# Node values moved from VectorE to GpSimd, the second norm moved into the pair tiles, the first tile's pair weights ahead of the scans

## The reference

```python
diff  = cg[:, :, None, :] - cg[:, None, :, :]
decay = exp(where(tri, diff, -1e30))
levels = floor(log2(s XOR t)) + 1, and 0 for s == t
lam_ts = Lam[t, head, levels[t, s]]          # Lam = softplus(Lp * dl)
scores = q_t . k_s / sqrt(64)
Y = (scores * decay * lam_ts) @ V
o = Y @ Wout.T + x, then a layer norm of o with ln_g, ln_b
```

## Time and profile before

| | |
|---|---|
| median of 3 runs | 1217.08 us (1216.16 to 1217.61) |
| profiled execution | 1215.93 us |
| its span | 1213.8 us |
| mean granted TensorE clock | 0.959 of full |
| TensorE busy | 1091.7 us |
| VectorE busy | 1004.4 us |
| ScalarE busy | 691.8 us |
| GpSimd busy | 310.4 us |

### The profile page before, as it was taken

One profiled execution on the slowest core, in us unless ns is written; L12 is line 12 of the kernel. 1 busy time (PEld: TensorE's weight loads), 2 busy tenths in 40 slices (PEclk: granted clock), 3 DMA queues, 4 the chain that ended last, 5 costly groups with the idle time before them and its releaser, 6 DMA issues.

```text
span 1213.8 us, 18006 instructions
## 1 busy us (share of the span) xinstructions
PE 1091.7 (90%) x5756; PEld 665.3 (55%) x5756; DVE 1004.4 (83%) x2141; ACT 691.8 (57%) x1366; POOL 310.4 (26%) x197
## 2 busy tenths in 40 slices
PE   5799989998998989899998989989898998989872
PEld 3455646555564655556465555646555564655641
DVE  4688897979979797997979799797979979797677
ACT  4483845738375573837557283755728375572761
POOL 0050320504114050411405041140504114050273
PEclk9899989899999999999899999999999999999885
DMA  3000000000000000000000000000000000001136
GB/s 133 9 9 10 1 18 9 17 9 0 17 9 17 9 17 9 0 17 9 17 9 17 9 0 17 9 17 9 17 9 0 17 9 17 9 17 54 67 101 203
DMA packets 32562, 28.64 MB, mean 24 GB/s; under 512 B 1568, under 2 KB 26144, under 8 KB 32288
## 3 DMA queue, kind: packets, MB, share of 16 engines
q1 hardware_dynamic: 32544, 28.42, 7.2%
HBM read 16.09 MB, written 12.32 MB: 23 GB/s over the span
## 4 chain that ended last, share of the span: by engine, by line
PE 45%; DVE 37%; issue 11%; ACT 5%; DMA 1%; DVEq 0%; ACTq 0%; SPq 0%; POOLq 0%; POOL 0%
DVE ms L1256 6%; PE p L581 4%; PE p L619 3%; DVE skip L1088 3%; PE p L544 3%; PE p L556 2%; PE p L570 2%; DVE pair L1329 2%; DVE nodesT L1265 2%; PE p L433 2%; PE p L394 2%; ACT vdw L849 2%; PE p L424 2%; DVE pair L1323 2%; DVE y L1168 2%
## 5 line engine op out<-in xcount | busy, mean ns | idle before, releaser
L1516 POOL TENSOR_TENSOR pair<-pair,cgt 128x2048 f32<-128x2048 f32 x16 | 58.4, 3647 | 772.5 <-DVE pair L1316 772.5
L858 ACT ACTIVATE gx<-p 128x512 f32<-128x512 f32 x256 | 143.4, 591 | 13.9 <-PE p L479 8.2
L477 PE MATMUL p<-x1Th,Gl 128*128 128x512 f32 x256 | 120.1, 469 | 4.0 <-ACT gx L858 4.0
L813 ACT ACTIVATE gelu<-p,bias_u 128x512 f32<-128x512 f32 x32 | 22.0, 687 | 151.3 <-PE p L424 151.3
L479 PE MATMUL p<-x1Th,Gh 128*128 128x512 f32 x256 | 102.1, 399 | 0.0
L478 PE MATMUL p<-x1Tl,Gh 128*128 128x512 f32 x256 | 101.8, 398 | 0.0
L1529 POOL TENSOR_TENSOR vp<-vdw,beta 128x384 f32<-128x384 f32 (+3 forms) x80 | 80.9, 1042 | 56.0 <-DVE beta L1308 56.0
L544 PE MATMUL p<-gx,x1T 128*32 128x512 f32 x512 | 77.2, 679 | 12.8 <-DVE pair L1333 12.0
L581 PEld LDWEIGHTS p<-vbd,pair 128*128 128x128 f32 x512 | 62.0, 191 | 42.9 <-issue 31.0
L1256 DVE TENSOR_TENSOR ms<-lam,K 128x64 f32<-128x64 f32 (+4 forms) x80 | 84.5, 1132 | 0.0
L394 PE MATMUL p<-xnT,MC 128*128 128x512 f32 x64 | 42.6, 756 | 46.4 <-DVE y L1161 46.4
(11 more groups left out here) (239 smaller groups left out, 2705.3 us busy)
## 6 DMA issues: line engine op xcount, KB each, us to landing
xin<-in_x SPq DMA_DIRECT2D x16, 256.0 KB, 2.8
hx_scratch<-vdw SPq DMA_DIRECT2D x16, 256.0 KB, 2.5
res_scratch<-res SPq DMA_DIRECT2D x15, 256.0 KB, 2.0
W<-in_weights SPq DMA_DIRECT2D x1, 1477.5 KB, 9.3
gx<-hx_scratch SPq DMA_DIRECT2D x5, 256.0 KB, 4.5
out<-gx SPq DMA_DIRECT2D x5, 256.0 KB, 2.7
gx<-in_weights SPq DMA_DIRECT2D x1, 1216.0 KB, 11.7
GT<-hx_scratch SPq DMA_DIRECT2D x4, 256.0 KB, 4.1
```

The costliest lines, as they stand in the source:

```text
L477: pe.matmul(head_bank(h)[:, :], tile(Gl, h), x1Th[:, :], start=True, stop=False)
L858: act.activation(tile(gx, h, T), head_bank(h)[:, :], ACT.Copy).then_inc(R["gx_copied"], 1)
```

## The change

- `pair_differences` and ScalarE's `pair_decay` work by tile, in four pieces each.
- Level 0 goes into the node values. The setup (`node_vectors`) makes `member` (query or key below the node), `rbit` and `own_coef`, and adds to `left` a row for the token itself. A new VectorE step `fold_own` combines level 0 with the levels 1 to 5 in `lam`, behind `lam_sum`. `own_level` and `self_lam` go, and with them the sum of L1329 in `pair_weights`.
- `node_lams` moves from VectorE to GpSimd: behind `pair_differences` and ahead of `level_values`, five products (1, 2, 4, 8, 16 columns) and a copy.
- `attention_out` writes into `skip` and not into `rs`. `norm2` moves from ahead of `node_rows` to behind `pair_weights(1)`.
- `pair_weights(0)` moves ahead of the scans, and TensorE's `pair_levels(0)` ahead of `left_halves`.

```diff
-        yt, ytT, ob = rs[:, 0:T], rs[:, T:2 * T], rs[:, 2 * T:3 * T]
+        yt, ytT, ob = rs[:, 0:T], rs[:, T:2 * T], skip
...
                     pair_scores(i, 0)
+                    pair_levels(i, 0)
                     left_halves(i)
-                    pair_levels(i, 0)
                     node_matrices(i)
...
+                for n in range(TILES):
+                    act.wait_ge(R["diff_ready"], 4 * i + n + 1)
+                    act.activation(tile(pair, n, 512), tile(pair, n, 512), ACT.Abs).then_inc(R["diff_abs"], 1)
+                for n in range(TILES):
+                    act.wait_ge(R["diff_abs"], 4 * i + n + 1)
+                    act.activation(tile(pair, n, 512), tile(pair, n, 512), ACT.Exp, scale=-1.0).then_inc(R["decay_ready"], 1)
...
                 if later(i):
                     act.wait_ge(R["m_ps"], 4 * i)
                 if later(i):
-                    act.wait_ge(R["n_ready"], i)
+                    act.wait_ge(R["ob_ready"], i)
+                    act.wait_ge(R["c_ready"], B if isinstance(i, int) else i)
...
+            def node_vectors():
...
+                step(dve.transpose(left_t[:, :], k("left")))
+                step(dve.tensor_reduce(member[:, :], view(left_t[:, :], "p (c n) -> p n c", c=4), AX.X, ALU.add))
+                step(dve.tensor_tensor(member[:, :], member[:, :], k("right"), ALU.add))
...
+                step(dve.scalar_tensor_tensor(own_coef[:, 0:5], ones_to[:, 1:6], -2.0, ones_to[:, 0:5], ALU.mult, ALU.add))
+                step(dve.tensor_copy(own_coef[:, 5:6], ones_to[:, 5:6]))
+                left = view(k("left"), "p (c s) -> p c s", c=4)
+                step(dve.scalar_tensor_tensor(left, spread(k("own_chunk").unsqueeze(2), [128, 4, CHUNK]), k("diag", 31, 32),
+                                              left, ALU.mult, ALU.add))
...
+            def fold_own(i):
 
                 dve.wait_ge(R["lam_ready"], i + 1)
                 if later(i):
-                    dve.wait_ge(R["lev_ps"], 4 * i)
+                    dve.wait_ge(R["nodes_ready"], i)
...
+                own = view(lam_own[:, :], "p (m l) -> p m l", l=6)
+                dve.tensor_tensor(own, spread(l[:, :, 0:1], [128, 64, 6]),
+                                  spread(own_coef[:, :].unsqueeze(1), [128, 64, 6]), ALU.mult).then_inc(R["own_steps"], 1)
+                dve.tensor_tensor(l[:, :, 1:6], l[:, :, 1:6],
+                                  spread(rbit[:, :].unsqueeze(1), [128, 64, 5]), ALU.mult).then_inc(R["own_steps"], 1)
+                dve.wait_ge(R["own_steps"], 2 * i + 2)
+                dve.tensor_tensor(l[:, :, 1:6], l[:, :, 1:6], own[:, :, 0:5], ALU.add).then_inc(R["lamx_ready"], 1)
...
             def pair_weights(i, n):
-                if n == 0:
-                    dve.wait_ge(R["decay_ready"], i + 1)
+                dve.wait_ge(R["decay_ready"], 4 * i + n + 1)
                 dve.wait_ge(R["lam_ps"], 4 * i + n + 1)
                 dve.tensor_tensor(tile(pair, n, 512), tile(pair, n, 512), P1[2][:, :], ALU.mult)\
                     .then_inc(R["dlam_ready"], 1)
 
-                if n == 0:
-                    dve.wait_ge(R["self_ready"], i + 1)
+                dve.wait_ge(R["s_ps"], 4 * i + n + 1)
                 dve.wait_ge(R["dlam_ready"], 4 * i + n + 1)
-                dve.tensor_tensor(tile(pair, n, 512), tile(pair, n, 512), tile(self_lam, n, 512), ALU.add)\
-                    .then_inc(R["lams_ready"], 1)
-                dve.wait_ge(R["s_ps"], 4 * i + n + 1)
-                dve.wait_ge(R["lams_ready"], 4 * i + n + 1)
                 dve.tensor_tensor(tile(pair, n, 512), tile(pair, n, 512), P1[1][:, :], ALU.mult)\
                     .then_inc(R["w_ready"], 1)
 
...
             def attention_out(i):
                 dve.wait_ge(R["wo_ps"], i + 1)
-                if later(i):
-                    dve.wait_ge(R["n_ready"], i)
+                dve.wait_ge(R["skip_ready"], i + 1)
...
                     lam_sum(i)
+                    fold_own(i)
...
-                    node_lams(i)
                 if j is not None:
                     scan_inputs(j)
                 if i is not None:
-                    if later(i):
-                        norm2(i - 1)
                     node_rows(i)
+                if i is not None:
+                    pair_weights(i, 0)
                 if j is not None:
                     scans(j)
                 else:
                     cell_out()
-                if i is not None:
-                    pair_weights(i, 0)
                 if j is not None:
                     top1(j)
                 if i is not None:
                     own_heads(i, 0)
                     pair_weights(i, 1)
+                    if later(i):
+                        norm2(i - 1)
...
+            def node_lams(i):
+
+                pool.wait_ge(R["lamx_ready"], i + 1)
+
+                if later(i):
+                    pool.wait_ge(R["c_ready"], B if isinstance(i, int) else i)
+                if later(i):
+                    pool.wait_ge(R["lev_ps"], 4 * i)
+                l = view(lam[:, :], "p (m l) -> p m l", l=LEVELS)
+                own = view(lam_own[:, :], "p (m l) -> p m l", l=6)
+                nd = view(nodes[:, :], "p (m n) -> p m n", n=NODES)
+                at = 0
+                for level in range(5, 0, -1):
+                    count = CHUNK >> level
+                    pool.tensor_tensor(nd[:, :, at:at + count], spread(l[:, :, level:level + 1], [128, 64, count]),
+                                       spread(member[:, at:at + count].unsqueeze(1), [128, 64, count]), ALU.mult)
+                    at += count
+                pool.tensor_copy(nd[:, :, at:at + 1], own[:, :, 5:6]).then_inc(R["nodes_ready"], 1)
...
-                pw = view(pair[:, :], "p (m t) -> p m t", t=CHUNK)
-                pool.tensor_tensor(pw, pw, spread(cgt[:, :].unsqueeze(2), [128, 64, CHUNK]), ALU.subtract)\
-                    .then_inc(R["diff_ready"], 1)
+                for n in range(TILES):
+                    pw = view(tile(pair, n, 512), "p (m t) -> p m t", t=CHUNK)
+                    pool.tensor_tensor(pw, pw, spread(cgt[:, H * n:H * n + H].unsqueeze(2), [128, H, CHUNK]), ALU.subtract)\
+                        .then_inc(R["diff_ready"], 1)
...
                 pair_differences(i)
+                node_lams(i)
                 level_values(i)
-                own_level(i)
```

More of the change, by code:

```diff
@@ L168, in build @@
         nodesT = sb("nodesT", TILES * 512)
-        self_lam = sb("self_lam", TILES * 512)
+        lam_own = sb("lam_own", 64 * 6)
+        member = sb("member", NODES)
+        left_t = sb("left_t", 128)
+        rbit = sb("rbit", 5)
+        ones_to = sb("ones_to", 6)
+        own_coef = sb("own_coef", 6)
         vp = sb("vp", 2048)
@@ L198, in build @@
         P1 = [psum(f"p1_{n}") for n in range(5)]
[L200 removed]
+        names = """loaded heads_loaded folded basis setup_ps setup_ev setup_done G_ps G_ready Gh_ready Gl_ready
             gates_xh_ready gates_xl_ready
@@ L1067, in before, with step @@
                 dve.wait_ge(R["setup_done"], 3)
+            def node_vectors():
+                steps = [0]
+                def step(ins):
+                    steps[0] += 1
+                    ins.then_inc(R["basis"], 1)
+                    dve.wait_ge(R["basis"], steps[0])
+                step(dve.transpose(left_t[:, :], k("left")))
[4 more added lines that the diff above has]
+                    count = CHUNK >> level
+                    step(dve.tensor_reduce(rbit[:, level - 1:level], k("right", at, at + count), AX.X, ALU.add))
+                    at += count
+                step(dve.memset(ones_to[:, 0:1], 1.0))
+                for level in range(1, 6):
+                    step(dve.tensor_tensor(ones_to[:, level:level + 1], ones_to[:, level - 1:level],
+                                           rbit[:, level - 1:level], ALU.mult))
+                step(dve.scalar_tensor_tensor(own_coef[:, 0:5], ones_to[:, 1:6], -2.0, ones_to[:, 0:5], ALU.mult, ALU.add))
[3 more added lines that the diff above has]
+                                              left, ALU.mult, ALU.add))
             def heads_low_part():
@@ L1468, in stages @@
                     heads_low_part()
+                    node_vectors()
                 if j is not None:
```

32 lines of the change are left out of this document (7 added, 25 removed).

## The result

The changed kernel takes 1249.82 us (median of 4 runs, 1247.48 to 1251.67) against 1217.34 us of the kernel before on the same chip. The ratio is 1.025, with a 95% interval of 1.0225 to 1.0275. The prediction was 1219.0 us, with a range up to 1234: it was wrong. The profiled execution took 1250.59 us, of which the span is 1248.8.

The account below looks back on a forecast made before the run. The prediction took the moment VectorE issues scan_inputs as the limit, with w(0) second. Its terms, 1.3 - 4 - 2 - 8.5 + 9 + 2.7 + 3.4, sum to +1.9 us: 1219.0 us, range 1191 to 1234.

Parts of the forecast that it names:

- step 9: ScalarE's Abs and Exp in four pieces add perhaps 0.8 us, vbd ready near 586.2: costs nothing.
- step 4: VectorE's alpha products wait in turns for GpSimd's node products; scan_inputs starts near 581.6 against 581.71: -2 us over 15 passes.
- Step 6: norm2 and L1329's additions leave the queue, pair_weights(0) comes earlier; TensorE's w(0) waits at L544 go: -8.5 us.
- Step 7: With pair_levels(0) ahead of left_halves, node_matrices wait 0.6 us for ScalarE's last copy in each of 15 passes: +9 us.
- Step 8: pair_levels(0) asks for nodesT earlier; with the clock up TensorE waits 0.9 us, in three passes: +2.7 us.
- Step 11: Pass 1's 6.66 us stall before the MC matmul shrinks to the other passes' 2.96, plus some clock: -4 us.
- step 10: At the start, node_vectors puts 17 waited-for instructions, 3.8 us, where 2.6 us are idle: +1.3 us.
- Step 3: GpSimd's node values, five products and a copy, take 4.5 us, from 575.0 to 579.5; bounds 3.7 and 5.3 us.
- the second rival: GpSimd's nodes are slower, 5.3 us, so beta, stats2 and scan_inputs come 0.8 us later: 1233 us, chance 0.20.
- The first rival: Node instructions do not hold VectorE in turns; scan_inputs starts at 578.4: 1188 us, or 1203 for half; chance 0.30.
- Step 5: GpSimd's level values start at 580.4, end by 585.2, before TensorE comes to left_halves after 586: hidden.
- Step 12: At the end, norm2(14) comes later, GpSimd's end sums start near 1181, and attention_out(15) is issued at 1205.7: +3.4 us.

Follow-up runs that it names:

- Experiment 1: Changed kernel with ScalarE's rstd2(i-1) moved from behind heads(12, 14) to behind own_values: 1215.43 us, ratio 0.998.
- experiment 5: Experiment 2's kernel with level_weights directly behind lam_sum on VectorE, ahead of fold_own: 1206.12 us, ratio 0.9891.
- experiment 9: Experiment 2's kernel with level_weights cut in two: beta products ahead of fold_own, alpha products and their product with e4 behind top1: 1188.23 us, ratio 0.9744.
- experiment 10: Experiment 9's kernel with ScalarE's Abs and Exp as one instruction each: 1186.79 us, ratio 0.9739.
- experiment 12: Experiment 10's kernel with the beta products between fold_own and delta, and ScalarE's own values behind its left_halves copies: 1187.79 us, ratio 0.9743.
- Experiment 8: Kernel before with only norm2(i-1) moved behind pair_weights(1), its sum written to skip's buffer, additions of self_lam kept: 1268.82 us, ratio 1.0406.
- experiment 3: Changed kernel with pair_levels(0) back behind left_halves on TensorE: 1273.80 us, ratio 1.0454.
- experiment 11: Experiment 2's kernel with pair_levels(0) back behind left_halves on TensorE and pair_weights(0) back behind the scans on VectorE: 1237.44 us, ratio 1.0154.
- experiment 2: Changed kernel with stats2(i-1) ahead of level_weights on VectorE: 1203.37 us, ratio 0.988.
- experiment 4: Changed kernel with ScalarE's Abs and Exp as one instruction of 2048 elements each instead of four of 512: 1234.96 us, ratio 1.0122.
- experiment 6: Experiment 5's kernel with level_values ahead of node_lams, left_halves ahead of pair_levels(0), and the scans ahead of pair_weights(0): 1272.47 us, ratio 1.0443.
- experiment 7: Experiment 6's kernel with ScalarE's Abs and Exp as one instruction each: 1251.19 us, ratio 1.0276.

## Why the prediction was wrong

The step that failed is step 9, "nothing" for ScalarE, and with it the end of step 4: step 4 gave the moment of stats2 and asked only what stands behind it on VectorE. stats2 ends 5 us later in the pass by the numbers of that very step, rstd2 on ScalarE waits for it, and the last heads copies, Abs, Exp, the own values and the left_halves copies are queued behind rstd2. "Vbd ready near 586.2" came out as 604.12 less 13.64, 590.5. Experiment 1 shows that this is the miss: without it the change takes 1215.43 us, and the forecast's own range was 1213 to 1225. Its passes take 4.4 us less than those of the kernel before, where the forecast's terms for the passes (steps 4, 6, 7, 8 and 11) sum to -2.8. Of the other terms only the start (step 10) was off by more than 2 us in the change.

Step by step, in the frame of the prediction (the changed kernel's times less 13.64):

- Steps 1 and 2 (pieces, fold_own): folded values forecast at 574.9; the nodes start at 574.91.
- Step 3 (nodes in 4.5 us): 4.9 with the copy, above the 4.7 from which the second rival was to decide. It did not: scan_inputs was at 581.76, as forecast at 581.6.
- Step 4 (turns): alpha ends at 579.65 (forecast 579.4), beta is ready at 580.4 (580.4). The stall before the MC matmul is 2.83 us instead of 2.96. The first rival, no turns, is out by the row of 4.38 us and by experiments 5 and 9. The rule that the prediction weighed, that a VectorE instruction with two SBUF inputs contends with a GpSimd instruction that reads SBUF (the Trainium skill, SBUF — State Buffer, Who interferes with whom), agrees with this row and with the 0.77 us of the same products beside an idle GpSimd.
- Step 5 (level values hidden): right in the change. It is the limit of experiments 9, 10 and 12.
- Step 6 (-8.5 us): the w(0) waits are gone. Experiment 8 shows how narrow the room in the tiles is: in the kernel before, with its additions of self_lam, the same move costs some 50 us.
- Step 7 (0.6 us before node_matrices, +9): the wait is there, 9.3 us in all, but as the price of the third part it is mis-sized: undoing it costs 24 us (experiment 3), or 34 with its counterpart on VectorE (experiment 11), because pair_levels(0) fills a gap and feeds pair_weights(0).
- Step 8 (nodesT late): 0.8 us in the change, forecast 2.7; left_halves and ScalarE took its place. In experiment 1, with ScalarE out of the way, it is 7.2 us in 7 waits, so the term was too small.
- Step 10 (start, +1.3, measured +4.8): the 17 steps take 3.8 us as forecast. In experiment 2 sum0 follows the last of them at once:

```profile
49.16 0.35 DVE L1099 SCALAR_TENSOR_TENSOR K<-K 128x128 f32<-128x128 f32 x1
49.55 0.69 DVE L1225 TENSOR_TENSOR x<-p,xin 128x512 f32<-128x512 f32 x1
```

  In the changed kernel's profile they are hidden behind TensorE, whose granted clock is 0.66 from 40 to 55 us against 0.92 before, and sum0 waits 2.57 us for it. The kernels of experiments 1 to 7 and 9 to 12 have this same start code, and their first sum0 lies between 49.5 and 54.3. What sets the clock there is open.
- Step 11 (pass 1, -4): -2.1, as the pass has the new loss too; in experiment 1 it is -4.3.
- Step 12 (end, +3.4): +3.2. TensorE now waits 9.1 us for ScalarE's copy in project_out, but is done before VectorE comes to attention_out(15), as forecast. The first end sum starts 46.8 us later, 15.0 of them beyond the shift of the last sum0:

```profile
1212.73 2.50 POOL L1590 TENSOR_TENSOR y<-y,sp 128x512 f32<-128x512 f32 x2
```

The second stretch of low clock was not foreseen either. It came with the two waits for ScalarE; in experiment 1, where the wait at left_halves is gone, L535 takes 3.83 us in every pass whose rows are whole.

## What to carry to other kernels

Where a result comes later, follow it to every engine that waits for it, and price what is queued behind each waiting instruction there, however small that instruction is: here an instruction on 4 columns held over 10 us of ScalarE's work. Beside a busy GpSimd a tiny VectorE instruction with two SBUF inputs costs as much as GpSimd's instruction (4.38 us for four that take 0.77), so keep those instructions out of that stretch and put there what reads SBUF once: the transpose L1298 takes its 2.30 us beside the level values too. The parts of a change are not a sum: moving norm2 alone costs some 50 us, undoing the third part on experiment 2 costs 34, and the kernel that has both with stats2 ahead is 14 us faster than the one before.

## What the runs showed of the hardware

- The same gap is followed by a low clock in one pass and not in the next. In experiment 2 TensorE idles 2.0 us before the second MC matmul in each loop pass; in the 3 us behind that the granted clock is 1.00 in the pass at 572.20 and 0.57 in the pass at 641.92. With a second gap close behind the first it is low in most passes: in experiment 11 (2.01 and 1.85 us of idle time, 4.9 us apart) 0.52 behind the second, the 1.2 GHz level, and 1.9 us or more for the first two left_halves matmuls in 10 of 14 loop passes, where they take 1.12 at 2.4 GHz.
- The granted clock early in the program differs between kernels whose code up to that place is the same, 0.65 to 0.98 in the stretch from 40 to 55 us; the two at hand, 0.66 and 0.89 (the change and experiment 2), lie 4.7 us apart at the first sum0.
- Four pieces of 512 elements on ScalarE take 2.18 us where one instruction of 2048 takes 1.91.
